# Spreading the first scan over twelve tiles, and places and scatter placed behind the norm

## The reference

```python
x = x + 0.5 * ffn(layernorm(x))       # router over 8 experts, top 2, plus 2 shared experts, inner size 640
x = x + ssm(layernorm(x))
x = x + 0.5 * ffn(layernorm(x))       # the same weights again

# ssm: D_INNER 256, D_STATE 16, a scan over the 256 positions of each of the 4 sequences
h = exp(dt_t * A) * h + dt_t * B_t * x_t
y_t = sum_n h * C_t + D * x_t
```

## Time and profile before

| | |
|---|---|
| median of 3 runs | 547.87 us (546.45 to 549.91) |
| the profiled execution | 546.11 us, span 544.2 us |
| PE, DVE, POOL, ACT busy | 522.5, 327.8, 230.5, 156.9 us |
| mean granted PE clock | 0.993 |
| first scan, first to last DVE half state | 174 to 251 us |
| second scan, the first DVE half state | 314 us |

### The profile page before, as it was taken

One profiled execution on the slowest core, in us unless ns is written; L12 is line 12 of the kernel. 1 busy time (PEld: TensorE's weight loads), 2 busy tenths in 40 slices (PEclk: granted clock), 3 DMA queues, 4 the chain that ended last, 5 costly groups with the idle time before them and its releaser, 6 DMA issues.

```text
span 544.2 us, 11101 instructions
## 1 busy us (share of the span) xinstructions
PE 522.5 (96%) x4386; PEld 422.4 (78%) x4387; DVE 327.8 (60%) x654; ACT 156.9 (29%) x336; POOL 230.5 (42%) x208
## 2 busy tenths in 40 slices
PE   8999999999979999999979999999997999999996
PEld 7998997458958888447979788964487999954695
DVE  3843526422555999997686399999768232522224
ACT  1111122221117445443202643554421011222210
POOL 1041100322303999995453189999700540000031
PEclk9999999999999999999989999999999999999999
DMA  7986993912204445540321436556100230210012
GB/s 225 398 322 227 394 381 133 316 60 59 70 11 130 114 136 144 152 118 25 105 68 69 118 101 121 133 145 154 34 21 2 98 88 29 78 40 13 20 55 74
DMA packets 41991, 67.72 MB, mean 124 GB/s; under 512 B 5041, under 2 KB 24753, under 8 KB 41937
## 3 DMA queue, kind: packets, MB, share of 16 engines
q1 hardware_dynamic: 29968, 40.75, 25.7%
q10 hardware_dynamic: 8400, 16.12, 8.0%
q0 software_dynamic: 3568, 10.10, 5.5%
HBM read 48.74 MB, written 18.22 MB: 123 GB/s over the span
## 4 chain that ended last, share of the span: by engine, by line
PE 53%; DVE 15%; POOL 14%; issue 10%; DMA 4%; ACT 2%; POOLq 0%; SPq 0%; DVEq 0%; ACTq 0%
PE ps L513 18%; PE ps L528 10%; PE ps L538 10%; POOL region L954 7%; PE ps L551 6%; POOL xnt L968 5%; DVE ps L1035 3%; DMA xg_rows<-region,pos 2%; PE ps L661 2%; PE ps L562 2%; DVE hb L990 2%; PE ps L713 1%; PE ps L683 1%; DMA region<-yg_rows,ypos 1%; PE ps L557 1%
## 5 line engine op out<-in xcount | busy, mean ns | idle before, releaser
L513 PEld LDWEIGHTS ps<-xt,w_gu 128*128 128x128 f32 x1360 | 156.3, 192 | 13.7 <-ACT xt L770 5.6
L513 PE MATMUL ps<-xt,w_gu 128*128 128x128 f32 x1360 | 161.3, 277 | 4.5 <-DVE xres L1005 2.8
L990 DVE SCALAR_TENSOR_TENSOR hb<-hb,ps 128x640 f32<-128x640 f32 x68 | 55.5, 816 | 134.3 <-ACT hb L752 134.0
L538 PE MATMUL ps<-w_dn,hb 128*128 128x256 f32 x520 | 122.1, 383 | 0.0
L538 PEld LDWEIGHTS ps<-w_dn,hb 128*128 128x128 f32 x520 | 96.0, 193 | 11.2
L752 ACT ACTIVATE hb<-ps 128x640 f32<-128x640 f32 x68 | 47.4, 698 | 173.6 <-PE ps L513 167.2
L513 PE MATMUL ps<-xnt,w_gu 128*128 128x128 f32 x720 | 86.3, 279 | 5.5 <-DVE xres L1005 5.5
L513 PEld LDWEIGHTS ps<-xnt,w_gu 128*128 128x128 f32 x720 | 84.8, 195 | 7.5 <-DVE xres L1005 5.9
L968 POOL TENSOR_TENSOR xnt<-xnt,hh 128x512 f32<-128x512 f32 x64 | 81.8, 1278 | 1.3 <-DVE hh L1040 1.3
L935 POOL DMA_INDIRECT region<-yg_rows,ypos x32 | 30.6, 955 | 116.4 <-DMA yg_rows<-ob 94.8
L1035 DVE TENSOR_TENSOR_SCAN ps<-ps,region 128x512 f32<-128x512 f32 x64 | 78.2, 1223 | 0.9 <-POOL region L954 0.7
(11 more groups left out here) (104 smaller groups left out, 329.7 us busy)
## 6 DMA issues: line engine op xcount, KB each, us to landing
bcb<-bc_rows SPq DMA_DIRECT2D x22, 512.0 KB, 5.0
region<-bc_rows SPq DMA_DIRECT2D x10, 512.0 KB, 5.3
xg<-xg_rows SPq DMA_DIRECT2D x34, 128.0 KB, 3.6
w_gu<-in_wg ACTq DMA_DIRECT2D x6, 640.0 KB, 7.1
w_gu<-in_wu ACTq DMA_DIRECT2D x6, 640.0 KB, 8.5
w_dn<-in_wd ACTq DMA_DIRECT2D x6, 640.0 KB, 9.2
yg_rows<-ob SPq DMA_DIRECT2D x20, 128.0 KB, 4.1
xg_rows<-bcb SPq DMA_DIRECT2D x1, 2176.0 KB, 15.2
```

What stands on the lines that cost most here:

```text
L513: last = nc.tensor.matmul(gup(p)[:, c * P:(c + 1) * P], w_gu4[:, e, k, c * P:(c + 1) * P], x, start=(k == 0), stop=(k == KC - 1))
L538: ins = nc.tensor.matmul(outp(p), hb[:, p, c * P:(c + 1) * P], w_dn4[:, e, c, :], start=(c == 0), stop=(c == IC - 1))
L990: nc.vector.scalar_tensor_tensor(out=h, in0=h, scalar=1.0, in1=gup(p)[:, 0:I], op0=ALU.add, op1=ALU.mult).then_inc(s_a, 1)
```

## The change

SHARES replaces PER_TILE: the first scan (of half 0, beside segment 1) is dealt out over twelve tiles with 2, 3, 3, 2, 3, 3, ... half states; the second keeps 2 and ten times 3. All but one of a tile's half states go ahead of its body, one behind it; the first tile has both behind it. In SCHEDULE the end of the first scan, Y 0, N P 2, O 1, G 1 and T P 2 move one tile later. The places become a step of their own. In segments 0, 1 and 3 it directly follows R2; in segment 2, R2 is followed by the whole combine of segment 1, N A 1 and tile 34, and then come the places and both parts of the scatter.

```diff
 def half_states(first, n, part):
 
-    a = PER_TILE * (n - first) - 1
-    a, b = (a, a + 2) if part == 0 else (a + 2, a + PER_TILE)
-    if n == first:
-        a, b = (0, 0) if part == 0 else (0, 2)
-    return range(a, b)
+    share = SHARES[segment(first) - 1]
+    a, count = sum(share[:n - first]), share[n - first]
+    ahead = 0 if n == first else count - 1
+    return range(a, a + ahead) if part == 0 else range(a + ahead, a + count)
...
-PER_TILE = 3
+SHARES = [[2, 3, 3] * 4, [2] + [3] * 10]
...
-    ("N", "P", 0), ("T", "P", 0), ("R1", 0), ("start",), ("R2", 0), ("S", 0, 0), ("S", 0, 1),
+    ("N", "P", 0), ("T", "P", 0), ("R1", 0), ("start",), ("R2", 0), ("places", 0), ("S", 0, 0), ("S", 0, 1),
...
-    ("scan", S1 + 2, S1 + 13, 0), ("first", S1 + 13), ("Y", 0), ("N", "P", 2), ("second", S1 + 13),
-    ("O", 1), ("G", 1), ("first", S1 + 14), ("T", "P", 2), ("second", S1 + 14), ("R1", 2),
-    ("first", S1 + 15), ("R2", 2), ("S", 2, 0), ("second", S1 + 15), ("C", 1, 0, 2),
-    ("tiles", S2 - 1, S2), ("C", 1, 2, TT), ("N", "A", 1), ("S", 2, 1),
-    ("tiles", S2, S2 + 1), ("first", S2 + 1), ("T", "A", 1), ("second", S2 + 1), ("X1", 1),
+    ("scan", S1 + 2, S1 + 14, 0), ("first", S1 + 14), ("Y", 0), ("N", "P", 2), ("second", S1 + 14),
+    ("O", 1), ("G", 1), ("first", S1 + 15), ("T", "P", 2), ("second", S1 + 15), ("R1", 2),
+    ("tiles", S2 - 1, S2), ("R2", 2), ("C", 1, 0, TT), ("N", "A", 1), ("tiles", S2, S2 + 1),
+    ("places", 2), ("S", 2, 0), ("S", 2, 1), ("first", S2 + 1), ("T", "A", 1), ("second", S2 + 1), ("X1", 1),
...
                 nc.vector.tensor_copy(tot[:, :, :].rearrange("p t e -> p (t e)"),
                                       bank7[:, TT * E:2 * TT * E]).then_inc(s_rkc, 1)
+
+            def places(s):
                 dve.wait_ge(s_rkc, s + 1)
...
                     route_rows(step[1])
+                elif kind == "places":
+                    places(step[1])
                     if step[1] == 1:
```

More of the change, by code:

```diff
@@ L132 @@
 SCHEDULE = [
-    ("N", "P", 0), ("T", "P", 0), ("R1", 0), ("start",), ("R2", 0), ("S", 0, 0), ("S", 0, 1),
+    ("N", "P", 0), ("T", "P", 0), ("R1", 0), ("start",), ("R2", 0), ("places", 0), ("S", 0, 0), ("S", 0, 1),
     ("tiles", 0, 6), ("N", "P", 1), ("tiles", 6, 8), ("T", "P", 1), ("tiles", 8, 9), ("R1", 1),
-    ("tiles", 9, 10), ("R2", 1), ("S", 1, 0), ("S", 1, 1), ("tiles", 10, S1 - 2), ("O", 0), ("G", 0),
+    ("tiles", 9, 10), ("R2", 1), ("places", 1), ("S", 1, 0), ("S", 1, 1), ("tiles", 10, S1 - 2), ("O", 0), ("G", 0),
     ("tiles", S1 - 2, S1 - 1), ("C", 0, 0, 2), ("tiles", S1 - 1, S1), ("C", 0, 2, TT), ("N", "A", 0),
     ("tiles", S1, S1 + 1), ("first", S1 + 1), ("T", "A", 0), ("second", S1 + 1), ("X1", 0),
-    ("scan", S1 + 2, S1 + 13, 0), ("first", S1 + 13), ("Y", 0), ("N", "P", 2), ("second", S1 + 13),
-    ("O", 1), ("G", 1), ("first", S1 + 14), ("T", "P", 2), ("second", S1 + 14), ("R1", 2),
-    ("first", S1 + 15), ("R2", 2), ("S", 2, 0), ("second", S1 + 15), ("C", 1, 0, 2),
-    ("tiles", S2 - 1, S2), ("C", 1, 2, TT), ("N", "A", 1), ("S", 2, 1),
-    ("tiles", S2, S2 + 1), ("first", S2 + 1), ("T", "A", 1), ("second", S2 + 1), ("X1", 1),
+    ("scan", S1 + 2, S1 + 14, 0), ("first", S1 + 14), ("Y", 0), ("N", "P", 2), ("second", S1 + 14),
+    ("O", 1), ("G", 1), ("first", S1 + 15), ("T", "P", 2), ("second", S1 + 15), ("R1", 2),
+    ("tiles", S2 - 1, S2), ("R2", 2), ("C", 1, 0, TT), ("N", "A", 1), ("tiles", S2, S2 + 1),
+    ("places", 2), ("S", 2, 0), ("S", 2, 1), ("first", S2 + 1), ("T", "A", 1), ("second", S2 + 1), ("X1", 1),
     ("scan", S2 + 2, S2 + 13, 1), ("first", S2 + 13), ("Y", 1), ("N", "P", 3), ("second", S2 + 13),
     ("first", S2 + 14), ("T", "P", 3), ("second", S2 + 14), ("O", 2), ("R1", 3),
-    ("first", S2 + 15), ("R2", 3), ("S", 3, 0), ("S", 3, 1), ("G", 2), ("second", S2 + 15),
+    ("first", S2 + 15), ("R2", 3), ("places", 3), ("S", 3, 0), ("S", 3, 1), ("G", 2), ("second", S2 + 15),
     ("tiles", S2 + 16, S3 + 6), ("C", 2, 0, TT), ("tiles", S3 + 6, S3 + 13), ("O", 3), ("G", 3),
```

## The result

| | before | changed |
|---|---|---|
| median of 10 runs each | 547.86 us | 550.75 us |
| lowest, highest | 544.73, 549.91 | 548.78, 554.89 |
| profiled execution, its span | 546.11, 544.2 | 548.78, 546.7 |
| mean granted PE clock | 0.993 | 0.990 |

The ratio of the changed kernel to the one before is 1.0078, with a 95% interval of 1.0052 to 1.0104: 2.9 to 5.7 us slower, 4.3 in the middle. 551.6 was forecast.

A forecast was written before the change was run, and what follows sets the result against it. PE was busy 522.5 of 544.2 us. The late scatter was to start the second scan 3.4 us later, plus 0.3 for the second load: 547.87 + 3.7 = 551.6 us, range 548 to 556 (0.84).

The forecast's parts named there:

- gate-up 31: PE's first half of tile 31, after the first scan: starts at 245.1 instead of 248.2, 3.1 us saved.
- wait of gate-up 33 for drain 31: New PE stall of 1.5 us behind the first scan: drain 31 done on DVE only at 265.7, after norm P 2.
- wait of gate-up 36 for drain 34: PE stall of 1.6 us, until drain 34 is done on DVE at 290.5; replaces the old 2.79 us stall.
- places end: Segment 2's places on DVE, behind combine, norm A, hidden 35 and drain 34: end at 297.0 instead of 280.1.
- PE's wait ahead of gate-up 39: PE, free at 315.2, stands until 322.9 because the second scan starts late: 7.7 us.
- both gates: Late scatters hold POOL's store of B and C to 308.9 and SP's load, whose own scatter wait ends by 310.3.
- The spread scan: First scan over twelve tiles, POOL and DVE just below PE's time: full saving of 3.1 us.
- the rival that gave it no effect: Spreading the first scan brings nothing, POOL's 20.0 too close to 20.5: 3.1 us later, 554.7; chance 0.12.
- The gain from X1 being early: X1 ends at 301.5 instead of 305.4, PE 3.9 us ahead; rival that the scan keeps it: 544.0, chance 0.13.
- the rival of a slow scatter: Fourth scatter of segment 2 lands in 6.6 us, not 2.4: +4.2 on top, 555.8; chance 0.15.
- The second slot: Second load for the second scan lands 7.7 behind its issue, at 319.1; POOL wants it about 318.8: 0.3 us more.
- the rival that charged 2 us for it: Clock ramp behind PE's long wait before the second scan's tiles isn't hidden: +2 us, 553.6; chance 0.08.

The follow-up runs named there:

- e3: Changed kernel without the second four scatters of segment 2, so two of its four row blocks aren't routed: 0.9980 of the kernel before, 547.34 us.
- e4: Changed kernel with segment 2's second four scatters behind X1, the store of B and C ahead of them: 1.0102 of the kernel before.
- e6: Changed kernel with both edits, of e4 and e5, so only four scatters precede the store and the loads: 0.9986 of the kernel before.
- e7: e6 with tile 31's drain put ahead of norm P 2 on DVE: 0.9951 of the kernel before.
- e5: Changed kernel with the second scan's third B and C slot moved so SP waits for four scatters only: 1.0103 of the kernel before.
- a1: Changed kernel, unedited, timed again (the second comparison): 1.0134 of the kernel before, median 555.19 us.
- e2: Changed kernel's new order, but the first scan over eleven tiles as before: 1.0141 of the kernel before.
- e1: Changed kernel's spread first scan, but places and first scatter behind R2 as in the kernel before: 1.0053 of that kernel.

## Why the prediction was right

Its steps, with the times of after put on the scale of before (2.07 added):

| step | forecast | measured |
|---|---|---|
| gate-up 31 | 245.1 | 245.2 |
| wait of gate-up 33 for drain 31 | 1.5 | 1.69 |
| wait of gate-up 36 for drain 34 | 1.6 | 1.27 |
| places end | 297.0 | 297.4 |
| X1 ends | 301.5 | 302.0 |
| first scatter | 297.5 | 298.3 |
| store of B and C | 308.9 | 310.2 |
| SP's first load | 310.9 | 312.5 |
| first input product | 316.0 | 317.7 |
| first scan instruction | 317.3 | 319.1 |
| PE's wait ahead of gate-up 39 | 7.7 | 8.99 |

**The mechanism** is the one that was named: e3, and e4 to e6 together, show both gates. The forecast held SP's wait for the scatter to be the earlier one by 0.6 us; by the estimate under e4 it was, by 0.2. The spread scan gave its 3.0 us in full, against the rival that gave it no effect. The gain from X1 being early was there (3.4 us of the 3.9 forecast) and was thrown away, since the scan no longer waits for X1. With both gates opened, e6 and e7 start the scan 1.6 and 2.2 us ahead of before, so even there it isn't had in full.

**The terms that were mis-sized** are small and all err to one side: the first scan instruction comes 1.8 us later than forecast. The places themselves are 0.4 late; the chain behind them makes the rest. The first scatter came 0.94 behind the places, not 0.5: 281.03 - 280.10 = 0.9 was the right row, and I went below it. The eight scatters to the store took 11.85, not 11.4; two of them took 1.41 and 1.02 instead of 0.97, why isn't shown. The store took 2.29 to SP's load, not 2.0 (e5 shows the same 2.29 without the wait for the last four scatters, so it is the store's). The load with its release took 5.3, not 5.1, and the first input to the scan 1.36, not 1.27. For the scatters the forecast used the quickest of the three pieces of eight in the kernel before: segment 0's took 42.66 + 0.96 - 28.18 = 15.4 us and segment 1's 112.30 + 0.97 - 99.28 = 14.0, with longer waits for the landing of the first four (before, POOL, first and last of each piece and the fifth):

```profile
28.18 1.05 POOL L917 DMA_INDIRECT xg_rows<-region,pos  x1 [16.69 <-DVE table L1135]
...
38.84 0.96 POOL L917 DMA_INDIRECT xg_rows<-region,pos  x1 [5.78 <-DMA xg_rows<-region,pos]
...
42.66 0.96 POOL L917 DMA_INDIRECT xg_rows<-region,pos  x1 [0.30 <-issue]
...
99.28 1.01 POOL L917 DMA_INDIRECT xg_rows<-region,pos  x1 [31.82 <-DMA xg_rows<-bcb]
...
108.48 0.97 POOL L917 DMA_INDIRECT xg_rows<-region,pos  x1 [4.35 <-DMA xg_rows<-region,pos]
...
112.30 0.97 POOL L917 DMA_INDIRECT xg_rows<-region,pos  x1 [0.30 <-issue]
```

The measured 11.85 is close to the quickest, so the choice was good, and the rival of a slow scatter falls.

**The second slot.** It landed 8.5 us behind its issue, not 7.7. POOL waits 1.21 us for it at 319.34, and DVE 0.46. From gate-up 39 to the mixed gate-up that waits for L768 it then takes 367.98 - 322.60 = 45.38, against 44.83 before. The forecast had 0.3 for this.

**The slow clock** behind the long wait was taken as hidden. It fell as expected:

```profile
322.60:324.60 2.00, 2.00 (x9) 2.00 (x10) 1.51 (x3) 0.78 (x2) 2.00 (x3) 0.50 0.76 154
```

(a stretch of after: its length, PE, PEld, DVE, ACT, POOL busy, then the granted clock, 0.50, which is 1.2 GHz; gate-up 39 takes 7.07 us, and 5.09 before.) But e6, whose PE had idled 2.13 us there and whose gate-up 39 ran its first 32 matmuls in 3.84, needs 363.11 - 317.82 = 45.29 for the same distance. The other kernels agree: 44.9 to 45.5 in the five kernels with a slow clock there (after, a1, e2, e4, e5), 45.2 to 45.4 in the three with the clock at 1.00 (e3, e6, e7). So the ramp is hidden, and the rival that charged 2 us for it falls. The Trainium skill (TensorE: Matmul & The Clock Gate, Part 1: The HAM clock gate), which has an idle PE start again at the lower clock, is borne out by the row; what it costs is told only by the work that PE waits for next.

**What the forecast left out.** At the mixed tiles of the second scan 0.4 us more is lost (381.84 - 367.98 = 13.86 against 377.75 - 364.29 = 13.46), with 0.3 us ahead of L526 put down to issue. All kernels with the late places show 13.8 to 13.9, e1 13.50. Its cause stays open.

**The sum.** The scan starts 5.2 late, and by the last gate-up that waits for a drain (424.49) the changed kernel is 6.2 us behind. It ends only 546.7 - 177.60 - (544.2 - 179.67) = 4.6 behind, because the clock didn't fall in that wait: by the gate-up that follows it is (427.65 - 177.60) - (425.10 - 179.67) = 4.6 behind as well. In a1's profile the clock fell there, as before, and it ends 552.9 - 181.29 - 364.5 = 7.1 behind. So the mechanism costs 6 us or more by these traces, the forecast was 1.8 short at the scan's start, and that +3.7 lies so near the first comparison's +4.3 is in part luck: the second comparison gave +7.4.

## What to carry to other kernels

When a step is moved later, follow it through every in-order queue that it is moved ahead of: here the scatter cost nothing on its own engine, but it came to stand in front of the store and the loads that start the next stage. Two gates that open at nearly the same time, a queue's order and a wait on a semaphore, must both be moved: each edit alone measured as nothing, and together they gave 6.4 us. Where the moved chain becomes the bound, small misses of its links add up, here to 1.4 us over the five behind the places, so the sum needs a range of its own; the slowest row isn't the cure, since 15.4 us for the scatters would have been 3.5 too many.

## What the runs showed of the hardware

**The same idle time, another clock.** Before the last eight matmuls of gate-up 51, PE idles 2.73 to 2.76 us in every one of these profiles. Before and after (clock is the last but two):

```profile
420.39:422.39 2.00, 2.00 (x9) 2.00 (x10) 0.68 (x1) 0.00 (x0) 1.70 (x2) 0.50 0.16 66
```

```profile
424.49:425.49 1.00, 1.00 (x9) 1.00 (x10) 0.67 (x1) 0.00 (x0) 1.00 (x1) 1.00 0.00 0
```

The eight matmuls behind it take 2.08 us in four of the kernels (before, a1, e2 and e7), 1.16 in two (after and e5), and 1.38 to 1.66 in the other four. So behind one and the same idle time the granted clock was 0.50 in some runs and 1.00 in others, 0.9 us (2.08 less 1.16) on these eight matmuls. Idle times of 9 us made it fall each time (after, a1, e2, e4, e5), and idle times of 1.87 to 2.19 us at the same place left it at 1.00 (e3, e6, e7).

**The part that nobody changed** varies by 5.9 us from profile to profile: the start of gate-up 22. So a distance inside a trace says more here than the span, and it is likely, though not shown, that this also widens the intervals, which are 0.6 to 1.1% wide for the eight kernels.
